# A fused decoder layer: the low part of the first attention's queries made once and spread by GpSimd, with all orders and PSUM banks laid anew

## The reference

```
attn1:  q, k, v = x @ W_attn            16 heads of 8 channels, causal
        att = q k^T / sqrt(8)
        p   = polymax(att)              x > 0: x^2 + 1;  -100 <= x <= 0: 1 - x/100;  else 0;  all / 1000
        x1  = layernorm(x + (p v) @ W_proj)
attn2:  16 heads of 64 channels, keys and values from the context, softmax
        x2  = layernorm(x1 + attn @ WO + bO)
ffn:    router over 16 experts (128x128 each), softmax, the best 6 renormalised to gates
        x3  = layernorm(x2 + sum_e gate_e * (x2 @ expert_e))
```

## Time and profile before

| what | value |
|---|---|
| median of the runs | 1046.49 us (1043.28 to 1046.57, 3 runs) |
| profiled execution | 1040.84 us, span 1038.7 us |
| busy, of the span: PE / PEld | 995.9 us (96%) / 862.0 us (83%) |
| busy: DVE / ACT / POOL | 969.5 (93%) / 757.5 (73%) / 391.8 us (38%) |
| mean granted TensorE clock | 0.994 |
| chain that ended last | PE 80%, DVE 11%, issue 4%, ACT 2% |
| of it, lines | DVE qm_lo L921 3%, DVE kp_lo L928 2% |

### The profile page before, as it was taken

One profiled execution on the slowest core, in us unless ns is written; L12 is line 12 of the kernel. 1 busy time (PEld: TensorE's weight loads), 2 busy tenths in 40 slices (PEclk: granted clock), 3 DMA queues, 4 the chain that ended last, 5 costly groups with the idle time before them and its releaser, 6 DMA issues.

```text
span 1038.7 us, 44351 instructions
## 1 busy us (share of the span) xinstructions
PE 995.9 (96%) x16344; PEld 862.0 (83%) x16344; DVE 969.5 (93%) x3176; ACT 757.5 (73%) x1606; POOL 391.8 (38%) x681
## 2 busy tenths in 40 slices
PE   5999999999999999999999999999999999999984
PEld 4888888888888888888888888888888888888873
DVE  5989999999999999999999999999999999999885
ACT  5987778777778777778777778777778787777641
POOL 1433333433333433333434333434333444333331
PEclk9999999999999999999999999999999999999997
DMA  5100100000000000000000000000000000000000
GB/s 169 43 18 13 28 17 25 25 25 11 24 15 25 25 25 13 22 15 25 25 25 23 13 15 25 25 25 25 10 15 25 25 25 25 10 20 13 13 7 10
DMA packets 29576, 25.14 MB, mean 24 GB/s; under 512 B 2528, under 2 KB 24544, under 8 KB 29536
## 3 DMA queue, kind: packets, MB, share of 16 engines
q1 hardware_dynamic: 29536, 24.57, 8.4%
HBM read 20.37 MB, written 4.19 MB: 24 GB/s over the span
## 4 chain that ended last, share of the span: by engine, by line
PE 80%; DVE 11%; issue 4%; ACT 2%; SPq 1%; POOL 1%; DMA 0%; DVEq 0%; ACTq 0%; POOLq 0%
PE ps_B L430 62%; PE ps_S L430 10%; PE ps_B L557 6%; DVE qm_lo L921 3%; DVE kp_lo L928 2%; DVE stats L780 1%; DVE ps_B L935 1%; PE ps_B L516 1%; PE ps_B L580 1%; SPq L396 1%; DVE sums L856 1%; DVE logit L880 0%; DVE rowmax L799 0%; DVE mv L786 0%; DMA xT<-in_x_t 0%
## 5 line engine op out<-in xcount | busy, mean ns | idle before, releaser
L856 DVE SCALAR_TENSOR_TENSOR sums<-ps_B,gate,sums 128x128 f32<-128x128 f32 x896 | 236.9, 341 | 2.2 <-PE ps_B L430 2.2
L997 POOL TENSOR_TENSOR p<-p,rowinv 128x1024 f32<-128x1024 f32 x64 | 121.9, 1905 | 193.6 <-DVE rowinv L812 193.6
L987 POOL TENSOR_TENSOR rstd<-mv,ln_eps_tile 128x2 f32<-128x2 f32 x96 | 18.7, 195 | 383.0 <-DVE mv L786 383.0
L627 ACT ACTIVATE q2T<-ps_B 128x512 f32<-128x512 f32 x128 | 76.0, 596 | 77.3 <-PE ps_B L430 74.1
L653 ACT ACTIVATE relu<-ps_B 128x512 f32<-128x512 f32 x128 | 73.1, 599 | 73.2 <-PE ps_B L430 72.8
L430 PE MATMUL ps_B<-wo_sb,oT 128*128 128x128 f32 x1024 | 122.8, 278 | 0.0
L627 ACT ACTIVATE p2T<-ps_B 128x512 f32<-128x512 f32 x128 | 76.9, 603 | 59.5 <-PE ps_B L557 58.1
L430 PEld LDWEIGHTS ps_B<-wo_sb,oT 128*128 128x128 f32 x1024 | 116.7, 192 | 2.4 <-DVE sums L856 0.3
L430 PE MATMUL ps_B<-ex_hi,x2T_hi 128*128 128x512 f32 x256 | 110.4, 431 | 1.2 <-POOL x2T_lo L971 0.8
L735 ACT ACTIVATE x<-ps_B,shift,rstd 128x128 f32<-128x128 f32 x192 | 78.4, 469 | 37.7 <-POOL shift L992 37.7
L430 PE MATMUL ps_B<-ex_hi,x2T_lo 128*128 128x512 f32 x256 | 102.0, 399 | 0.0
(11 more groups left out here) (122 smaller groups left out, 2913.7 us busy)
## 6 DMA issues: line engine op xcount, KB each, us to landing
xT<-in_x_t SPq DMA_DIRECT2D x32, 256.0 KB, 2.7
cT<-in_ctx_t SPq DMA_DIRECT2D x32, 128.0 KB, 2.3
...
```

Source lines behind the costliest of these rows:

```text
L627: return nc.scalar.activation(dst, src, ACT.Copy, scale=scale)
L856: done = V.scalar_tensor_tensor(after, ps[BANK[f"FF{4 * r + q}"]][:, C * e:C * e + C], gate[:, r, 4 * q + e:4 * q + e + 1], before, ALU.mu ...
L997: G.tensor_tensor(weights, weights, rowinv[:, r].unsqueeze(2).broadcast_to([P, H, T]), ALU.mult).then_inc(p2_ready, 1)
```

## The change

1. ScalarE's queries_hi makes one more copy: q_hi, the scaled, unmasked high part (128x256).
2. VectorE's queries_lo makes one unmasked low part q_lo from PSUM and q_hi, in place of four masked ones, and frees Q's bank.
3. GpSimd gets a step, qmask: one product of q_lo, spread over the four copies, and head_mask, spread over the tokens, 128x1024 elements, into qm_lo. It waits for Q's bank to be emptied.
4. S1 waits for qmask (a semaphore of its own, qm_lo_ready) in place of Q's bank, and for K's.
5. All orders, and nearly all banks, are other ones.

```diff
 JOBS = [
-    ("V2_0", "B2", "l2"), ("S2_0", "S", "l2"), ("Y", "B4", "l1"), ("X2T", "B3", "ff"), ("Q", "B1", "s1"),
-    ("PR", "B5", "l1"), ("LG", "B3", "ff"), ("K", "B2", "s1"), ("V2_1", "B4", "l2"), ("V2_2", "B3", "l2"),
-    ("V2_3", "B0", "l2"), ("S2_1", "S", "l2"), ("S1_0", "B2", "s1"), ("V", "B1", "s1"), ("S1_1", "B3", "s1"),
-    ("X1T", "B0", "l1"), ("K2_0", "B4", "l1"), ("K2_3", "B1", "l1"), ("Q2_3", "B0", "l1"), ("K2_1", "B5", "l1"),
-    ("K2_2", "B1", "l1"), ("PT0b", "B4", "l2"), ("Q2_2", "B0", "l1"), ("FF0", "B2", "ff"), ("PT0a", "B5", "l2"),
-    ("FF4", "B4", "ff"), ("FF1", "B1", "ff"), ("FF5", "B5", "ff"), ("AC0", "S", "l2"), ("PT1a", "B0", "l2"),
-    ("PT1b", "B4", "l2"), ("FF2", "B2", "ff"), ("FF6", "B0", "ff"), ("S1_2", "B3", "s1"), ("FF3", "B4", "ff"),
-    ("FF7", "B1", "ff"), ("S1_3", "B5", "s1"), ("AC1", "S", "l2"), ("WO0", "", "l2"), ("WO1", "B0", "l2"),
-    ("Q2_1", "B2", "l1"), ("Q2_0", "B1", "l1"),
+    ("V2_2", "B4", "l2"), ("Q", "B5", "s1"), ("S2_0", "S", "l2"), ("X2T", "B0", "ff"), ("K", "B1", "s1"),
+    ("Y", "B2", "l1"), ("V2_3", "B4", "l2"), ("PR", "B2", "l1"), ("LG", "B3", "ff"), ("V2_0", "B0", "l2"),
+    ("S1_0", "B5", "s1"), ("V2_1", "B3", "l2"), ("S1_1", "B1", "s1"), ("S2_1", "S", "l2"), ("V", "B3", "s1"),
+    ("X1T", "B4", "l1"), ("K2_1", "B2", "l1"), ("K2_0", "B0", "l1"), ("K2_2", "B3", "l1"), ("PT0b", "B5", "l2"),
+    ("K2_3", "B2", "l1"), ("FF4", "B0", "ff"), ("PT0a", "B5", "l2"), ("FF1", "B4", "ff"), ("Q2_0", "B2", "l1"),
+    ("FF0", "B1", "ff"), ("AC0", "S", "l2"), ("FF5", "B2", "ff"), ("FF2", "B3", "ff"), ("PT1b", "B5", "l2"),
+    ("FF6", "B1", "ff"), ("PT1a", "B0", "l2"), ("FF7", "B5", "ff"), ("S1_2", "B2", "s1"), ("FF3", "B4", "ff"),
+    ("S1_3", "B0", "s1"), ("AC1", "S", "l2"), ("WO0", "", "l2"), ("WO1", "B1", "l2"), ("Q2_1", "B3", "l1"),
+    ("Q2_3", "B5", "l1"), ("Q2_2", "B2", "l1"),
 ]
 DVE_ORDER = """
-    row_max0 less_max0 projected logits stats1 gate0 var1 gate1 queries_lo gate2 keys_lo0 gate3 keys_lo1 gate4
-    row_sum0 gate5 row_max1 gate6 row_inv0 x1_lo gate7 allow0 gate8 less_max1 gate9 pieces0 gate10 p1_0 gate11
-    allow1 gate12 gate13 row_sum1 gate14 row_inv1 gate15 pieces1 weigh0 p1_1 weigh1 weigh2 weigh3 stats3 allow2 var3
-    allow3 pieces2 pieces3 attended stats2 var2 p1_2 p1_3
+    row_max0 queries_lo less_max0 keys_lo0 keys_lo1 projected logits stats1 gate0 var1 gate1 row_sum0 gate2 gate3
+    row_inv0 gate4 allow0 gate5 row_max1 gate6 pieces0 gate7 gate8 p1_0 less_max1 gate9 allow1 gate10 x1_lo gate11
+    pieces1 gate12 p1_1 gate13 gate14 row_sum1 gate15 row_inv1 weigh0 weigh1 weigh2 weigh3 stats3 allow2 var3
+    pieces2 p1_2 attended stats2 var2 allow3 pieces3 p1_3
 """.split()
 ACT_ORDER = """
-    V2_0 Y X2T queries_hi exp0 logit_exp K V2_2 norm1 V2_1 V2_3 V relu0 x1_hi relu1 K2_0 K2_3 square0 Q2_3 K2_1 exp1
-    PT0b square1 K2_2 PT0a base3 Q2_2 PT1a PT1b AC0 relu2 relu3 AC1 square2 square3 Q2_1 Q2_0 norm3 norm2
+    queries_hi V2_2 K Y X2T V2_3 exp0 V2_0 logit_exp V2_1 relu0 norm1 square0 relu1 V K2_1 K2_0 square1 x1_hi K2_2
+    PT0b K2_3 exp1 PT0a Q2_0 base3 PT1b PT1a AC0 relu2 square2 relu3 AC1 square3 norm3 Q2_1 Q2_3 Q2_2 norm2
 """.split()
 POOL_ORDER = """
-    x2_hi root1 context_hi x2_lo context_lo shares0 shares1 root3 next_x_hi root2 next_x_lo bias_x1
+    qmask x2_hi root1 context_hi context_lo shares0 x2_lo shares1 next_x_hi next_x_lo root3 root2 bias_x1
 """.split()
...
                 def s1(last_unit):
                     units = range(last_unit - PARTS + 1, last_unit + 1)
-                    for job in latest(i, ("Q", "K"), [BANK[f"S1_{unit}"] for unit in units]):
-                        wait_emptied(pe, i, job)
+                    pe.wait_ge(qm_lo_ready, u + 1)
+                    if BANK["K"] not in [BANK[f"S1_{unit}"] for unit in units]:
+                        wait_emptied(pe, i, "K")
...
                 def queries_hi():
                     wait_full(act, i, "Q")
+                    copy(q_hi[:], ps[BANK["Q"]][:, 0:TOK], float(HD) ** -0.5)
                     for v in range(NV):
                         last = copy(qm_hi[:, :, v], ps[BANK["Q"]][:, 0:TOK].rearrange("p (b t) -> p b t", b=NB), query_mask[:, v:v + 1])
                     last.then_inc(qm_hi_ready, 1)
...
                 def queries_lo():
                     dve.wait_ge(qm_hi_ready, u + 1)
-                    if isinstance(i, int) and u == 0:
-                        dve.wait_ge(mask_steps, 2)
-                    for v in range(NV):
-                        last = V.scalar_tensor_tensor(qm_lo[:, :, v], ps[BANK["Q"]][:, 0:TOK].rearrange("p (b t) -> p b t", b=NB), query_mask[:, v:v + 1],
-                                                      qm_hi[:, :, v].bitcast(F32), ALU.mult, ALU.subtract)
-                    last.then_inc(emptied[BANK["Q"]], 1)
+                    V.scalar_tensor_tensor(q_lo[:], ps[BANK["Q"]][:, 0:TOK], float(HD) ** -0.5, q_hi[:].bitcast(F32), ALU.mult, ALU.subtract).then_inc(emptied[BANK["Q"]], 1)
...
+                def masked_lo():
+                    wait_emptied(pool, i, "Q")
+                    if isinstance(i, int) and u == 0:
+                        pool.wait_ge(mask_steps, 2)
+                    G.tensor_tensor(qm_lo[:], q_lo[:].bitcast(F32).rearrange("p (b t) -> p b t", b=NB).unsqueeze(2).broadcast_to([P, NB, NV, T]),
+                                    head_mask[:].unsqueeze(1).unsqueeze(3).broadcast_to([P, NB, NV, T]), ALU.mult).then_inc(qm_lo_ready, 1)
```

More of the change, by code:

```diff
@@ L114 @@
+        Q2_3@-1 K@0 Q2_2@-1 V2_3@0 queries_hi@0 Y@0 exp0@0 V2_0@0 V2_1@0 relu0@0 square0@0 norm1@0 V@0 K2_1@0 exp1@0 PT0b@0
+        K2_0@0 PT0a@0 x1_hi@0 K2_2@0 relu1@0 K2_3@0 AC0@0 PT1a@0 PT1b@0 square1@0 Q2_0@0 AC1@0 Q2_1@0 relu2@0 relu3@0
+        square2@0 square3@0 Q2_3@0 Q2_2@0 norm2@0
     """,
     "DVE": """
-        keys_lo0@-2 keys_lo1@-2 queries_lo@-2 allow0@-2 allow1@-2 pieces0@-2 pieces1@-2 p1_0@-2 p1_1@-2 heads_lo0@-2
-        allow2@-2 allow3@-2 pieces2@-2 pieces3@-2 p1_2@-2 p1_3@-2 keys_lo0@-1 queries_lo@-1 keys_lo1@-1 projected@-1
@@ L118 @@
-        heads_lo1@-2 stats1@-1 var1@-1 allow0@-1 pieces0@-1 allow1@-1 pieces1@-1 p1_0@-1 x1_lo@-1 p1_1@-1 heads_lo2@-2
-        allow2@-1 allow3@-1 pieces2@-1 p1_2@-1 pieces3@-1 p1_3@-1 row_max0@0 less_max0@0 projected@0 stats1@0 var1@0
-        queries_lo@0 keys_lo0@0 keys_lo1@0 row_sum0@0 row_inv0@0 row_max1@0 x1_lo@0 less_max1@0 allow0@0 pieces0@0
-        row_sum1@0 row_inv1@0 p1_0@0 allow1@0 pieces1@0 p1_1@0 allow2@0 allow3@0 pieces2@0 p1_2@0 pieces3@0 p1_3@0
-        attended@0 stats2@0 var2@0
+        queries_lo@-2 keys_lo0@-2 keys_lo1@-2 heads_lo0@-2 allow0@-2 allow1@-2 pieces0@-2 pieces1@-2 p1_0@-2 p1_1@-2
@@ new lines @@
+        allow2@-2 allow3@-2 pieces2@-2 pieces3@-2 p1_2@-2 p1_3@-2 keys_lo0@-1 queries_lo@-1 keys_lo1@-1 heads_lo1@-2
+        projected@-1 stats1@-1 var1@-1 heads_lo2@-2 allow0@-1 x1_lo@-1 pieces0@-1 allow1@-1 p1_0@-1 pieces1@-1 p1_1@-1
+        allow2@-1 pieces2@-1 p1_2@-1 allow3@-1 pieces3@-1 p1_3@-1 keys_lo0@0 keys_lo1@0 row_max0@0 queries_lo@0 less_max0@0
+        projected@0 stats1@0 var1@0 row_sum0@0 row_max1@0 allow0@0 row_inv0@0 pieces0@0 less_max1@0 p1_0@0 row_sum1@0
+        row_inv1@0 x1_lo@0 allow1@0 pieces1@0 p1_1@0 allow2@0 pieces2@0 p1_2@0 attended@0 stats2@0 var2@0 allow3@0 pieces3@0
@@ L130 @@
     "SP": """
-        store@NT-2 store@NT-1 x_rows@NT-2 context@NT-2 store@NT
+        store@NT-2 context@NT-2 x_rows@NT-2 store@NT-1 store@NT
     """,
     "PE": """
-        V2_0@NT-2 S2_0@NT-2 Y@NT-2 X2T@NT-2 V2_1@NT-2 PR@NT-2 V2_2@NT-2 V2_3@NT-2 LG@NT-2 S2_1@NT-2 K2_0@NT-2 FF0@NT-2
-        K2_3@NT-2 X1T@NT-2 K2_1@NT-2 PT0b@NT-2 K2_2@NT-2 Q2_3@NT-2 PT0a@NT-2 FF4@NT-2 FF1@NT-2 Q2_2@NT-2 AC0@NT-2 PT1a@NT-2
-        Q2_1@NT-2 FF5@NT-2 PT1b@NT-2 FF2@NT-2 FF6@NT-2 FF3@NT-2 AC1@NT-2 FF7@NT-2 WO0@NT-2 WO1@NT-2 Q2_0@NT-2 S2_0@NT-1
@@ L148 @@
     "DVE": """
-        row_max0@NT-2 less_max0@NT-2 projected@NT-2 stats1@NT-2 var1@NT-2 row_sum0@NT-2 logits@NT-2 row_inv0@NT-2 gate0@NT-2
-        gate1@NT-2 row_max1@NT-2 gate2@NT-2 gate3@NT-2 gate4@NT-2 less_max1@NT-2 gate5@NT-2 gate6@NT-2 gate7@NT-2 x1_lo@NT-2
-        gate8@NT-2 gate9@NT-2 gate10@NT-2 gate11@NT-2 row_sum1@NT-2 gate12@NT-2 gate13@NT-2 gate14@NT-2 row_inv1@NT-2
-        gate15@NT-2 weigh0@NT-2 weigh1@NT-2 weigh2@NT-2 weigh3@NT-2 stats3@NT-2 var3@NT-2 attended@NT-2 stats2@NT-2
@@ L158 @@
-        gate13@NT gate14@NT gate15@NT weigh0@NT weigh1@NT weigh2@NT weigh3@NT stats3@NT var3@NT
+        row_max0@NT-2 less_max0@NT-2 logits@NT-2 projected@NT-2 gate0@NT-2 stats1@NT-2 gate1@NT-2 var1@NT-2 row_sum0@NT-2
+        gate2@NT-2 gate3@NT-2 row_inv0@NT-2 row_max1@NT-2 gate4@NT-2 less_max1@NT-2 gate5@NT-2 gate6@NT-2 gate7@NT-2
+        gate8@NT-2 gate9@NT-2 x1_lo@NT-2 gate10@NT-2 gate11@NT-2 gate12@NT-2 gate13@NT-2 gate14@NT-2 gate15@NT-2
+        row_sum1@NT-2 row_inv1@NT-2 weigh0@NT-2 weigh1@NT-2 weigh2@NT-2 weigh3@NT-2 stats3@NT-2 var3@NT-2 attended@NT-2
@@ new lines @@
```

(5 more changed lines are left out.)

56 lines of the change are left out of this document (28 added, 28 removed).

## The result

The changed kernel took 1052.15 us (median of five runs, 1051.87 to 1052.63), the kernel before 1043.28 (five runs, 1041.0 to 1046.57). The ratio is 1.0078, with a 95% interval of 1.0054 to 1.0102: slower by 0.8%, which is small and yet outside its uncertainty. The forecast was no change at 1046, with a range of 1034 to 1056.

The account below looks back on a forecast made before the run. TensorE was taken as busy nearly throughout, VectorE almost full, with waits between them deciding. Stretches gave a 31.0 us turn, no change; 1040.8 - 0.9 + 0.5 = 1040.4 profiled, raised 5.65 to 1046; range 1034 to 1056.

Parts of the forecast that it names:

- A: Steady turn from S2_0 to S1: 5.29 to 5.45 us up to V2_1, then 0.77 to S1.
- B: Steady turn from S1 to PT1b: 12.6 us over VectorE and shares1, against 12.2 for TensorE alone.
- C: Steady turn from PT1b to the next S2_0: 12.4 us, before 12.21.
- the filling: First turns: 1.65 us of waiting for queries_lo replaced by hops, +1.2 us, half hidden, so +0.5 us.
- the port rule: VectorE instructions with two SBUF inputs and GpSimd SBUF reads exclude each other: B up to 0.3 longer, 1055; chance 0.03.
- queries_hi and norm2: ScalarE: queries_hi starts as Q ends; norm2 ahead of it counts only if more than 0.3 us late.
- a wait at V2_1 (logits): TensorE in the first stretch: V2_1 takes LG's bank and waits for logits, 0.04 to 0.20 us of new wait.
- VectorE's idle before row_max0: VectorE idles 1.8 us a steady turn before row_max0, waiting for S2_0, and is busy 28.7.
- VectorE's and GpSimd's path longer: Rival: V2_1 behind logits and PT1b behind shares1 both add; turn 31.3 to 31.4, 1055 us; chance 0.19.
- The product: GpSimd's new 128x1024 product takes 1.91 us and is hidden, with 1.3 us of slack before S1.
- The base: Sum made on the profiled execution, 1040.4 us, then raised by 5.65 to the median of runs, 1046.

Follow-up runs that it names:

- e8: Changed kernel with pieces1 and p1_1 behind row_inv1 on VectorE, and the banks of FF0, FF2 and FF6 changed to fit: 1069.43 us, ratio 1.027.
- e4: Changed kernel with VectorE's gates 7 and 8 behind p1_0 and gates 12 to 15 behind row_inv1: 1135.53 us, ratio 1.0892.
- e5: Changed kernel with only gates 7 and 8 moved behind p1_0 on VectorE: 1057.72 us, measured once.
- e9: e8 with half the columns of two of the four sets of weighted sums left out: 1051.86 us, measured once.
- e10: Changed kernel with half the columns of two of the four sets of weighted sums left out: 1048.51 us, measured once.
- e11: e8 with ScalarE also copying Y ahead of K in the steady order: 1069.97 us, ratio 1.0258.
- e7: Changed kernel with GpSimd's product made twice, the first time into a tile that nothing reads: 1069.83 us, measured once.
- e3: Changed kernel with X2T and Y copied before K on ScalarE, and projected and logits before the keys' low parts on VectorE: 1055.48 us, ratio 1.013.
- e6: Changed kernel with GpSimd's product over only one of the four sequences (256 of 1024 elements): 1052.68 us, measured once.
- e12: Changed kernel with, in the first tile's turn only, GpSimd's context_lo before root1 and VectorE's p1_0 before less_max1: 1052.64 us, measured once.

## Why the prediction failed

The forecast was no change, and the turn became 0.27 longer. The measured time lies inside the range, on the side of the rival that had a chance of 0.19. Of the three stretches, A came out 0.34 longer than the low end that I took (6.06), B 0.22 longer (12.5) and C 0.21 shorter (12.4). Two steps of the sum failed, the filling was sized from one old row, and a conclusion on the port rule was drawn from the wrong operation.

*queries_hi and norm2.* The prediction let queries_hi start as Q ends, and wrote that norm2 "stands ahead of it on ScalarE and would have to be more than 0.3 late to count". It was late by nearly 0.5. attended ran at 627.66, root2 ended at 630.37 on GpSimd, and norm2, queries_hi, V2_2's copy and K followed without a gap up to yT. I had placed the end of VectorE's stretch C ("they end just as WO1 does") and had not carried it on over stats2, root2 and norm2. The forecast also looked for a wait at V2_1 (logits) in stretch A and for none at PR, whose source yT has K in front of it. Measured: 6.40 against 6.06 to 6.32, with PR waiting 0.5 a turn and no wait at V2_1. That norm2 holds queries_hi is read from the timeline; no run put queries_hi ahead of norm2, so what that alone would give is not shown. VectorE's idle before row_max0 was 0.85 and not 1.8: it was busy 29.36 and not 28.7, and steps that feed each other stood 0.74 apart and not 0.6.

*Stretch B.* The path over VectorE and shares1 was given as 12.6, and it was 12.72: PT1b waits for shares1 as written, for some 0.45 on the weight loads (11.8 us in 26 turns). Of its parts only allow0 to row_inv1 was off by more than 0.05: 8.70 (607.45 to 616.15) and not 8.5. Not foreseen was PT0b's wait for p1_0, which costs some 0.4 of TensorE's lead before PT1b and nothing behind it (in e8, without shares1 in the way, the stretch is 12.54).

*Stretch C* was 12.19 and not 12.4 to 12.5. The sum of the three is 31.31, while I had taken 31.0 "since the wait between engines that are not backed up is nearer 0.06 than 0.22". The high ends were 31.5. The rival "VectorE's and GpSimd's path longer" gave 31.3 to 31.4 and 1055; its turn is what came. Of its two places one was right (PT1b behind shares1), the other was PR behind yT and not V2_1 behind logits.

*One loop through both places.* The prediction took the stretches one by one and asked in each which engine is last. They close into one loop, and the runs show it. From attended to the next S1 it takes 9.37 us in the changed kernel and 9.36 to 9.44 in e4, e5, e8, e9, e10 and e11, though their turns go from 31.18 to 34.08. From WO0 to attended it is 3.96 or 3.97 in all of them. So these two pieces have no slack in them: WO1, attended, stats2, root2, norm2, queries_hi, the copies of V2_2 and K, yT, PR, LG and the two V2 jobs, S1. Only e7, with its second product, has a longer first piece (9.78, 0.41 more, for a turn 0.40 longer). The third piece, S1 to WO0, is 17.98 in the changed kernel: 12.72 over relu0, VectorE up to row_inv1 and shares1 to PT1b, and 5.26 of TensorE behind it. The sum is 31.31. e3 took 0.30 from the first piece (9.07) and gave 0.40 to the third; e8 took 0.18 from the way to PT1b and gave 0.65 to what follows it; e10 took 0.13 from that. What VectorE works or saves beside this loop counts for nothing. In the order of before, yT started 1.35 behind norm2 on ScalarE (623.45 to 624.80); in the new one it is 3.57 (630.47 to 634.04), since queries_hi, V2_2's copy and K stand between. The forecast did not follow this path.

*The product.* 1.89 us forecast as 1.91, hidden, with 1.6 of slack forecast as 1.3: right, and e6 and e7 bear it out from both sides. No wait at V remained.

*The filling* was given +0.5 and cost 3.3 to 4.5, by the mark. The chain of 1.65 us for queries_lo went indeed. V of the second filling turn starts earlier (25.7, before 28.1), but only because S1 now stands behind it; the two together are issued by 28.2, before 28.7. In turn 0, the one before the first full turn, TensorE has issued both by 47.6, before 47.7: with the same jobs behind it in both: by this mark nothing is lost up to there. From V of turn 0 to V of turn 1 it is then 28.7 us, before 25.6. The waits of TensorE in that stretch add up to 3.3 us (0.67 and 0.59 above; 0.52 and 0.19 of "issue" ahead of the AC jobs; 0.43 for q2T; 0.87 of "issue" in Y); before, none there was longer than 0.44. e12 took two of them away and got nothing. I had read the earlier trace rows alone, which is a row of the old order; the new order's own first turns were not laid out. What would have to change there stays open.

*The Trainium skill.* The prediction weighed the page "SBUF — State Buffer" of the Trainium skill, section "Who interferes with whom", and set its rule aside ("so here it does not hold"), since a MATCH_REPLACE8 took 0.16 us in the middle of a share product. In the changed kernel this stayed without a price: gates 7 and 8 are again MATCH_REPLACE8 (609.95, 0.16, beside shares0 at 608.15 to 610.05). But e4's geps, a SCALAR_TENSOR_TENSOR with both inputs in SBUF, was held for the rest of the share product, 1.65 us for 0.16. There the rule agrees with the trace. The conclusion from one operation to all of them was wrong; it did no harm to the sum, since in the turns of the changed kernel no small operation of this kind lay beside a GpSimd product, and none took longer than before. Once, before the first turn, one did: w_qk_lo, with both inputs in SBUF, took 0.77 from 4.55 us, beside GpSimd's xT_lo (4.31 to 5.03), and 0.43 in the kernel before, from 5.60, when GpSimd was idle. Nor is it sure that MATCH_REPLACE8 was a case of the rule: a MATCH_VALUE_LOAD of 128x8 stands before it as an instruction of its own (609.88), so that the second operand may be read there and not by the replacement.

*The base.* The sum was for the profiled execution (1040.4) and then raised by 5.65 to the median of three runs, to 1046. Of five runs that median is 1043.28, so the raise hid 3 us of the miss: from 1043.28 the forecast would have been 1042.9, 9.3 too low. Against its own base, the profiled execution, it was 11.8 too low, part of which is the quick profiled run of before.
